# A vision tower with a routed expert layer: the first half routed in two groups, part of the gate moved to POOL, register reads gathered

## The reference

```python
g = _noisy_linear(x, W1_w, W1_b, W1_sw, W1_sb, eps_in1, eps_out1)
x_gate = g * jnp.tanh(jax.nn.softplus(g))
x_inner = _noisy_linear(x, W2_w, W2_b, W2_sw, W2_sb, eps_in2, eps_out2)
h = pos_encoding((x_gate * x_inner) @ W3_w.T + W3_b)         # 128 features
h = concatenate([cls_tok, h], axis=1)                         # 65 tokens an image
h = h + attention(layernorm(h))                               # 8 heads of 16
h = h + ffn(layernorm(h))
...
# attention: causal scores without softmax, normalised by their running mean and
# deviation (one mu and one s for each query and head), times v, then @ w_out + b_out
# ffn: two of eight experts for each token
logits = xf @ router_w
gate_vals, idx = jax.lax.top_k(logits, 2)
gates = jax.nn.softmax(gate_vals, axis=-1)
for e in range(8):
    hh = jax.nn.relu(xf @ w1[e] + b1[e]) @ w2[e] + b2[e]      # 128 -> 512 -> 128
    y = _layernorm(xf + hh, gamma[e], beta[e])
    out = out + jnp.sum(jnp.where(idx == e, gates, 0.0), axis=-1)[:, None] * y
```

## Time and profile before

| | us |
|---|---|
| median of 3 runs | 144.37 (144.24 to 144.65) |
| the profiled execution | 144.59 |
| its span, first to last instruction | 142.8 |
| PE busy | 130.9 (92%) |
| DVE busy | 104.4 (73%) |
| ACT busy | 72.9 (51%) |
| POOL busy | 57.3 (40%) |

### The profile page before, as it was taken

How to read it: one execution, slowest core, us unless ns; L and a number is a source line. 1 busy time by engine, 2 the same in 40 slices (tenths; PEclk the granted TensorE clock), 3 DMA queues, 4 the chain that set the end, 5 groups by cost and what they waited for, 6 DMA issues and landing times. The chain is left out here.

```text
span 142.8 us, 3886 instructions
## 1 busy us (share of the span) xinstructions
PE 130.9 (92%) x1210; PEld 114.2 (80%) x1210; DVE 104.4 (73%) x417; ACT 72.9 (51%) x214; POOL 57.3 (40%) x96
## 2 busy tenths in 40 slices
PE   7999899999999999889993899999999999999960
PEld 7944898788759898668930879999999999999950
DVE  1479999979988667778664029887878789988580
ACT  5534315834476531139900006887878977896000
POOL 8900000000000046775778131377677767680010
PEclk9999999999999999999555569999999999999999
DMA  4999399999993019611115477598999751015405
GB/s 117 263 457 418 156 387 414 404 339 274 278 270 113 5 17 333 255 50 56 45 56 101 179 166 221 133 317 277 243 334 311 239 163 41 21 33 167 175 0 149
DMA packets 16423, 28.47 MB, mean 199 GB/s; under 512 B 1793, under 2 KB 9878, under 8 KB 16276
## 3 DMA queue, kind: packets, MB, share of 16 engines
q1 hardware_dynamic: 13700, 25.43, 55.3%
q0 software_dynamic: 1152, 2.07, 4.3%
q10 hardware_dynamic: 1552, 0.73, 2.2%
HBM read 19.55 MB, written 12.09 MB: 222 GB/s over the span
## 5 line engine op out<-in xcount | busy, mean ns | idle before, releaser
L1457 PE MATMUL ps<-w_all,hid 128*128 (+1 forms) x184 | 24.7, 278 | 0.3 <-issue 0.2
L1457 PEld LDWEIGHTS ps<-w_all,hid 128*128 128x128 f32 x184 | 22.4, 192 | 1.0 <-issue 0.8
L503 POOL DMA_INDIRECT back<-kTm,xg x16 | 15.9, 997 | 12.2 <-ACT kTm L693 6.1
L684 ACT ACTIVATE hid<-ps,D 128x128 f32<-128x128 f32 x48 | 13.5, 362 | 13.7 <-PE ps L1438 13.7
L1150 PE MATMUL ps<-zeros 128*128 128x128 f32 x112 | 17.8, 312 | 2.9 <-POOL SQ L490 2.9
L1150 PEld LDWEIGHTS ps<-zeros 128*128 128x128 f32 x112 | 16.1, 222 | 3.9 <-POOL SQ L490 3.4
L471 POOL TENSOR_TENSOR ex<-e_base,dlt 128x5 f32<-128x5 f32 x1 | 1.2, 1207 | 44.8 <-DVE dlt L935 44.8
L464 POOL DMA_INDIRECT rows<-x2k,row_at x16 | 16.1, 1007 | 6.9 <-issue 5.0
L1054 DVE COPY xgT<-ps 128x128 f32<-128x128 f32 x23 | 6.7, 290 | 10.1 <-PE ps L1430 8.4
L1438 PE MATMUL ps<-xgT,D 128*128 128x128 f32 x96 | 12.8, 276 | 0.0
L684 ACT ACTIVATE hid<-ps,last_parts 128x128 f32<-128x128 f32 x44 | 12.4, 364 | 0.0
(11 more groups left out here) (236 smaller groups left out, 278.4 us busy)
## 6 DMA issues: line engine op xcount, KB each, us to landing
rows<-blank SPq DMA_DIRECT2D x8, 589.5 KB, 6.7
D<-pack SPq DMA_DIRECT2D x12, 386.0 KB, 5.2
last_parts<-pack SPq DMA_DIRECT2D x11, 386.0 KB, 4.8
pack<-w1b SPq DMA_DIRECT2D x1, 2064.0 KB, 15.6
w_all<-w SPq DMA_DIRECT2D x1, 2048.0 KB, 12.2
back<-zeros SPq DMA_DIRECT2D x1, 1152.0 KB, 9.0
xg<-rows SPq DMA_DIRECT2D x16, 65.5 KB, 3.0
xT_oT<-patches SPq DMA_DIRECT2D x2, 512.0 KB, 5.9
```

Source lines behind the costliest of these rows:

```text
L503: nc.gpsimd.indirect_dma_start(back, bass.IndirectOffsetOnAxis(ap=xg[j][:, P:P + 1].bitcast(U32), axis=0), z[j], None, bounds_check=P * K ...
L684: nc.scalar.activation(hid[j % 2][:, f, :], ps[:, 2 + 2 * (j % 2) + f // 2, f % 2 * P:(f % 2 + 1) * P], ACT.Relu, bias=packed[j % NW][:, H ...
L1457: last = mm(ps[:, 6 + j % 2, 0:P], hid[j % 2][:, f, :], w2_all[:, bass.ds(expert_j, 1), f, :].rearrange("p a n -> p (a n)"), start=(f == 0 ...
```

## The change

It has seven parts.

1. **Gate of the second half.** Of DVE's arithmetic, e limited, e + 2, n, half of n + 2, and g * n are now computed by five instructions on POOL, as soon as ACT has the exponential. DVE keeps the reciprocal and the last two products.
2. **DVE's constants** are filled between the two halves of the noisy weights instead of after the bias.
3. **Second half embedded earlier.** PE runs `embed(1)` ahead of `scores(0)` and of both `values`; DVE adds the positions before it masks `D`, and takes the statistics after it; `turn_norm(1)` is ahead of `weigh(1)`.
4. **The table `tab`** is no longer added by PE in each `sum_values`; POOL adds it to `h`, two instructions of 128 x 512, for which `residual_sums` waits (`h_tab`).
5. **Routing in groups.** The first half is turned and routed in two groups of two tiles; DVE chooses tiles 0 and 1 before `evict(3)` and 2, 3 and the class token after it. The reciprocal in part 0's softmax moves from a power on POOL to DVE. The last group's normalisation moves behind part 1's places. `keep_warm` counts change: none at place 4, five for three at place 5.
6. **Register reads.** PE waits for `slots_done` and reads all 18 expert numbers ahead of the warming products.
7. **SP** fetches the weight blocks of slots 5 and 6 after the rows of the last four slots, not before.

The core of the diff:

```diff
@@ SP
-            for j in range(FIXED, FIRST_ROWS):
-                load_pack(j)
+            expert_at(0)
             tile_at(FIRST_ROWS - FIXED)
...
             for j in range(SENT, SLOTS):
                 load_rows(sp, j, tile_at(j - FIXED))
+            for j in range(FIXED, FIRST_ROWS):
+                load_pack(j)
@@ POOL
+            second, last_half = slice(BANK, 2 * BANK), slice(BANK + BANK // 2, 2 * BANK)
+            pool.wait_ge(exp_done, 2)
+            nc.gpsimd.tensor_scalar(e_sb[:, second], e_sb[:, second], EXP_CAP, None, ALU.min).then_inc(mish_pool, 1)
+            pool.wait_ge(mish_pool, 1)
+            nc.gpsimd.tensor_scalar(gn_sb[:, second], e_sb[:, second], 2.0, None, ALU.add).then_inc(mish_pool, 1)
+            pool.wait_ge(mish_pool, 2)
+            nc.gpsimd.tensor_tensor(n_sb[:, second], gn_sb[:, second], e_sb[:, second], ALU.mult).then_inc(mish_pool, 1)
+            pool.wait_ge(mish_pool, 3)
+            nc.gpsimd.tensor_scalar(m_sb[:, last_half], n_sb[:, last_half], 2.0, None, ALU.add).then_inc(mish_pool, 1)
+            pool.wait_ge(gate_read, 2)
+            nc.gpsimd.tensor_tensor(gn_sb[:, second], g_sb[:, second], n_sb[:, second], ALU.mult).then_inc(mish_pool, 1)
...
+                nc.gpsimd.tensor_tensor(some, some, tab[:, :].unsqueeze(1).to_broadcast([P, CT, P]), ALU.add).then_inc(h_tab, 1)
...
-            nc.gpsimd.tensor_tensor(x2k[:, a:b, 0, P + 1], den[:, a:b], minus_one[:, a:b], ALU.pow).then_inc(first_gates, 1)
-            pool.wait_ge(first_gates, 3)
+            pool.wait_ge(first_recip, 1)
@@ ACT
             norm2_deviation(4)
-            twice(1)
             nc.scalar.activation(table_scrap[:, 3:4], zeros[:, 0:1], ACT.Exp)
             exp_gates(1)
-            copy_norm2(2)
+            twice(1)
+            copy_norm2(3)
@@ DVE
-            mish_start(1)
+            dve.wait_ge(mish_pool, 4)
             recip_of(1)
             mish_end(1)
+            embed_sum(1)
             evict(0)
+            embed_stats(1)
...
             normalise_group(1)
+            choose(0, GT, 1)
             evict(3)
-            choose(0)
+            choose(GT, CLS + 1, 2, 0)
             rank_tables(0)
             head_sums(2)
+            dve.wait_ge(first_gates, 2)
+            nc.vector.reciprocal(x2k[:, 0:CLS + 1, 0, P + 1], den[:, 0:CLS + 1]).then_inc(first_recip, 1)
...
-            choose(1)
-            normalise_group(3)
+            choose(*ROUTED[1], 3, 1)
             rank_tables(1)
             gates(1)
             places(1)
-            choose(2)
+            normalise_group(3)
+            choose(*ROUTED[2], 4, 2)
@@ PE
-                pe.wait_ge(tab_set, 1)
-                mm(ps[:, 6 + g % 2, GT * P:2 * GT * P], ident, tab[:, :].unsqueeze(1).to_broadcast([P, GT, P]),
-                   start=True, stop=False).then_inc(vsum_ps, 1)
...
+            embed(1)
+            scores(0)
             values(0)
             values(1)
-            scores(0)
-            embed(1)
             scores(1)
...
-            keep_warm(KEEP_WARM[4], 6)
+            turn_norm2(0)
+            sum_values(2)
+            route(0)
             scores(3)
-            turn_norm2(0)
+            turn_norm2(1)
             weigh(2, 0, GI // 2)
-            route(0)
+            route(1)
...
-            w2_experts = {}
+            pe.wait_ge(slots_done, 2)
+            w2_experts = list(range(FIXED))
+            for s in range(0, FREE, 4):
+                w2_experts += list(four_values(mybir.EngineType.PE, expert_of, s, EXPERTS - 1))
...
             pe.wait_ge(token_cols_set, 1)
             keep_warm(REWARM, 7)
-            pe.wait_ge(slots_done, 2)
```

More of the change, by code:

```diff
@@ L466, in dispatch @@
                         bounds_check=EXPERTS * SEG * P - 1, oob_is_err=False).then_inc(dispatched, 16)
+            pool.wait_ge(tab_set, 1)
+            for c in range(CHUNKS):
+                pool.wait_ge(xn_done, LN_TILES[c + 1][1] if c else 1 + CT)
+                some = h[:, CHUNK_AT[c]:CHUNK_AT[c] + CT, :]
+                nc.gpsimd.tensor_tensor(some, some, tab[:, :].unsqueeze(1).to_broadcast([P, CT, P]), ALU.add).then_inc(h_tab, 1)
             pool.wait_ge(rows_blank, 16 * (EXPERTS + 1))
@@ L718, in _, with attention_constants @@
                                            ).then_inc(f_abs_done, 1)
+            def attention_constants():
+                dve.wait_ge(after_iota, 2)
+                dve.wait_ge(vb_zero, 1)
+                dve.wait_ge(pick_zero, 1)
+                for half in range(2):
+                    rows64 = slice(PATCHES * half, PATCHES * (half + 1))
+                    nc.vector.tensor_scalar(after[rows64, :], after_raw[rows64, :], float(-PATCHES * half), None, ALU.is_ge
+                                            ).then_inc(after_set, 1)
+                    nc.vector.tensor_scalar(n_col[rows64, :], n_raw[rows64, :], float(-PATCHES * half), None, ALU.add
+                                            ).then_inc(after_set, 1)
+                    nc.vector.memset(vb[rows64, :, :, 2 * HD + half:2 * HD + half + 1], 1.0).then_inc(after_set, 1)
+                    nc.vector.memset(pick[rows64, half:half + 1], 1.0).then_inc(after_set, 1)
+                nc.vector.memset(h[:, CLS, :], 0.0).then_inc(consts_set, 1)
+                nc.vector.memset(acc[:, CLS, :], 0.0).then_inc(consts_set, 1)
             dve.wait_ge(f_parts, 2)
@@ L820, in mish_end, with embed_sum @@
                                                in1=gn_sb[:, sl], op0=ALU.add, op1=ALU.mult).then_inc(gT_done, 1)
-            def embed(c):
+            def embed_sum(c):
                 dve.wait_ge(h_ps, c + 1)
@@ L1304, in turn_norm2 @@
                 if c == 0:
-                    pe.wait_ge(acc_done, 2)
-                else:
+                    pe.wait_ge(v_done, 2 * GROUPS)
+                if c == 1:
+                    pe.wait_ge(x2T_done, 1)
+                if c == 2:
                     pe.wait_ge(D_done, GROUPS)
-                for i in range(PART_T[c]):
-                    t = PART_AT[c] + i
-                    pe.wait_ge(x2_done, PATCH_TILE[c] + i + 2)
-                    last = nc.tensor.transpose(ps[:, X2_BANK[c], i * P:(i + 1) * P], x2[:, t, :], ident)
+                for i in range(GT):
+                    pe.wait_ge(x2_done, GT * c + i + 2)
+                    at = X2_AT[c] + i * P
+                    last = nc.tensor.transpose(ps[:, X2_BANK[c], at:at + P], x2[:, GROUP_AT[c] + i, :], ident)
                 last.then_inc(x2T_ps, 1)
@@ L1316, in route @@
                 pe.wait_ge(x2T_done, c + 1)
-                pe.wait_ge(x2T_cls_done, 1)
+                if c == 1:
+                    pe.wait_ge(top_index, GT)
+                part = max(c - 1, 0)
                 router_wide = body_sb[:, BODY_AT["router"][0]:BODY_AT["router"][0] + SW]
-                for i in range(PART_T[c]):
-                    at = (PATCH_TILE[c] + i) * P
-                    last = mm(ps[:, LG_BANK[c], i * SW:(i + 1) * SW], x2T[:, at:at + P], router_wide, start=True, stop=True)
+                for i in range(GT):
+                    at = LG_AT[part] + (GROUP_AT[c] - ROUTED[part][0] + i) * SW
+                    last = mm(ps[:, LG_BANK[part], at:at + SW], x2T[:, (c * GT + i) * P:(c * GT + i + 1) * P], router_wide, start=True, stop=True)
                 if c == 0:
-                    mm(ps[:, LG_BANK[c], CLS * SW:(CLS + 1) * SW], zeros[:, :], router_wide, start=True, stop=True)
-                    last = mm(ps[0:1, LG_BANK[c], CLS * SW:(CLS + 1) * SW], x2T_cls[:, :], router_wide, start=True, stop=True)
+                    pe.wait_ge(x2T_cls_done, 1)
+                    at = LG_AT[0] + CLS * SW
+                    mm(ps[:, LG_BANK[0], at:at + SW], zeros[:, :], router_wide, start=True, stop=True)
+                    last = mm(ps[0:1, LG_BANK[0], at:at + SW], x2T_cls[:, :], router_wide, start=True, stop=True)
                 last.then_inc(logits_ps, 1)
```

136 lines of the change are left out of this document (64 added, 72 removed).

## The result

The changed kernel takes **149.37 us** (median of four executions), the kernel before 144.48 beside it. One of the four, of 151.90 us, was in the chip's slower state, and the others (148.07 to 149.50) give the ratio: 1.031, with an interval from 1.024 to 1.038. The kernel is slower, by 4.6 us between the two profiled executions. The forecast was 144.4 with 142.8 to 146.2. The profiled execution has a span of 147.4 us for its 149.23, where the one before has 142.8 for 144.59.

A forecast was written before the change was run, and what follows sets the result against it. Register reads were taken to set PE's start: `slots_done` at 73.3 plus 7.2 us, first product at 86.0 against 84.83, a loss of 1.2. The loop returns 1.1, so span 142.9 and time 144.4 us, range 142.8 to 146.2.

The forecast's parts named there:

- What bounds PE's start: Ahead of the warming: five reads in a row, 7.2 us (6.7 to 7.6), set PE's start at 80.5, not the dispatches.
- The first rival: At PE's start: reads cost only busy parts (4.4 us) or nothing, dispatches still decide; 141.7 or 140.3 us, chance 0.17.
- The loop: PE's expert loop of 23 slots: without register reads its visible stalls go, a gain of 1.1 us.
- `slots_done` at 73.3: End of routing, when slot numbers are ready: 73.3 in place of 73.80, a gain of 0.5 us (0 to 0.8).
- POOL beside DVE ... 0.3: Gate's first half: DVE slowed by POOL working beside it, a loss of 0.3 us, bounded by 0 and a third of 3.3.
- The constants' 0.45: Gate's first half: DVE's constants, moved from between bias and gate, fit into a wait; a gain of 0.45 us.
- Scores behind embed(1): Front on PE: first scores at some 27.3, before 27.84; only 0.1 to 0.3 us of gain reaches the mixing.
- Routing by groups: Choosing in two groups, and no table product on PE: the third group's residual sums come 2.6 us earlier.
- The last normalisation behind part 1's places: Late routing: part 1's places come 3.0 us earlier, but normalisation now stands behind them, leaving a gain of 0.8 us.
- The last dispatch: POOL's indirect stores: first starts at 53.6 instead of 56.09, last ends at some 75.2 instead of 78.02.
- The second rival: Gate's second half: POOL is late and PE stands in front of it, 2.2 us lost, 146.6 us; chance 0.21.
- The clock: PE's clock returns 5.9 us after the warming's start; earlier could gain 0.7 us, 1.5 later lose 0.7.

The follow-up runs named there:

- b1: The kernel before with all of PE's register reads moved between `slots_done` and the warming: 146.28 us, ratio 1.012.
- e2: The changed kernel with only the gate's second half put back on DVE, the new front order kept: ratio 1.062, with standstills.
- e4: The changed kernel with the last group's normalisation back ahead of the second part's rank tables, its transposes ahead of that part's ranks: 146.21 us, ratio 1.016.
- b2: The kernel before with five operations added on POOL, like the changed kernel's gate work, that nobody reads: ratio 1.016.
- e3c: The changed kernel with the front's order undone and the gate's second half left on POOL, on a chip without standstills: 149.29 us, ratio 1.032.
- e3b: The same kernel as e3c, run on a chip with standstills: 155.35 us beside 153.95 for the kernel before, no usable ratio.

## Why the prediction was wrong, step by step

- **What bounds PE's start** was right: the reads, not the dispatches. The first rival fell: reads in a row cost their full length (b1, and after). Their size was at the upper end and above it: 7.80, 7.73, 7.84 and 7.82 us from `slots_done` to the warming in four kernels, where I took 7.2 with 7.6 as the end. What was missing is in the reads themselves: in the changed kernel the first and the last of the five took 0.57 and 0.54 us where the earlier trace rows has 0.34, and the conversions came 0.29 apart on the mean, not 0.27. The steps before the first read and behind the last conversion are only 0.03 and some 0.1. It cost 0.6.
- **The loop**: 1.1 forecast, 1.1 measured.
- **`slots_done` at 73.3** is the step that failed; it came at 77.51, and by the text's own test (0.5 from 73.3) the forecast is wrong there. Most of these 4.2 us are in the front, which lost 3.3 against the kernel before where the forecast had no loss:
  - *"POOL beside DVE ... 0.3"*: the term that was mis-sized. It is 1.55 us in each of the seven kernels with POOL's gate work. The constants' 0.45 was gained beside it, but in this execution the exponential itself started 0.35 later than before (9.63 against 9.28), which takes most of that back: 1.55 - 0.45 + 0.35 is the queries' 1.45. I had bounded the term by a third of DVE's two-input time (1.1) and took a value near its low end, because in the earlier trace rows POOL was the one that suffered. The row that mattered most was no two-input operation at all but a copy of one partition that waited 0.86 us for POOL. And the other way to see it was the sum itself: the gate's second half left DVE with 1.5 us less to do, and its pairs began at 23.67 instead of 23.70.
  - *Scores behind embed(1)*: 0.1 to 0.3 forecast as a gain; 0.6 lost (8.06 against 7.43, in every kernel of the table but e2, where it is more). The second half's gated values came at 28.24 instead of 26.3, PE waited 0.80 for them, and the second scores then stood behind the values.
  - *A gap of 0.9 us in PE's sums of squares*, with 1.2 us to the next mark: not in the forecast in any form. 1.45 + 0.64 + 1.17, with 0.01 behind them, is the whole 3.27.
- **Routing by groups**: 2.6 forecast at the third group's residual sums, 1.5 measured. MAX8's wait of 1.56 became one of 0.52 and not zero, and the fourth group's scores came 0.37 later after the third's (2.93 against 2.56), behind the transposes and logits that now stand ahead of them on PE; I had counted nothing for those.
- **The last normalisation behind part 1's places**: 2.2 us given back forecast, some 2.1 measured (from +1.34 at those places, 68.46 against 67.12, to +3.48). Right, and e4 shows that it was a choice: the other order keeps 1.7 of it and costs POOL's ninth dispatch 0.4.
- **The last dispatch** ended at 79.80 and not at 75.2: the first was at 57.87 and not at 53.6, mostly for the front's sake, and the others follow it and the places. With the reads on the path it cost nothing.
- **The second rival** had the sign and two thirds of the size of the front's loss (146.6, from 2.2 us), but by another road: POOL was not late. Its gate work took 7.1 us (13.86 to 20.96), and DVE came for it at 23.67. The rival's upper end of 8.7 us has one product where POOL computes two; with both it would have been 10.6. The price that I named in passing, DVE losing a whole microsecond, was the mechanism; it deserved to be the rival's middle and the forecast's upper end.

- **The clock** came back 5.4 us after the warming's start in the kernel before (the granted clock is 1.00 from 84.6 on), not 5.9. The forecast hangs on this only through the range.

The range held none of this since its slow end summed only the forecast's own bounds (no gain at the slots, longest reads), though POOL's company had been bounded by a single row, far from the operations concerned.

## What to carry to other kernels

Work given to a second engine is to be priced at the first one too: what the first does meanwhile, down to the small copies, may wait for the second's instructions to end, and the relief may be gone before it is used. Reads of registers in a row are cheap only under a wait that is there anyway: count how many fit ahead of it (here three of five), and leave the others under queued matmuls. An order that saves a wait on one side should be followed to the next engine's queue: one normalisation behind three small steps cost 1.7 us by e4, more than the 1.5 that the routing by groups had gained.

## What the hardware did unexpectedly

- A DVE copy of one partition by 128 values took 1.06 us in place of 0.20 and ended 0.07 or 0.08 us after POOL's operation, in b2 and in all seven kernels with POOL's gate work.
- PE stopped for 0.2 to 2.2 us amid equal matmuls that waited for nothing, when a packet of an instruction queue (q8) came late beside a copy that filled the DMA queues; with the copy later the stop was gone. In all seven kernels with a stop PE went on 2.5 to 2.8 us after that packet's start. The same kernel had 1.09, none, and 2.23 us of it on three chips.
- On two of the four chips of the experiments PE, DVE and ACT stood still for 3 to 8 us in the routing of every kernel traced there, while POOL went on; the kernel before took 150.8 and 154.0 us there in place of 144.4. Why is open; no run here was made for it.
- PE's clock fell to the lower level in the front too: behind a stand of 3.02 us in e2 (0.50 granted from 32 to 34 us), behind one of 2.23 us in e3c (0.52 from 40 to 42), and in e3b (0.52 in the same stretch) with no stop ahead of it.
